# Gated cross-attention: probabilities and attended rows turned by VectorE and a DRAM round trip instead of by TensorE

## The reference

```
memory_proj = memory @ W_mem.T                          # 375 x 512 a batch
attn = softmax(x @ memory_proj.T / sqrt(512))           # 112 x 375
memory_context = attn @ memory_proj                     # 112 x 512
gate = sigmoid(concat(x, memory_context) @ W_gate.T + b_gate)
fused = x + gate * memory_context
out = fused * rsqrt(mean(fused^2) + 1e-6) * norm_w
```

## Time and profile before

| | us |
|---|---|
| median of 3 runs | 296.33 (296.28 to 297.29) |
| span of the profiled execution | 294.5 |
| TensorE busy | 287.4 |
| VectorE busy | 190.2 |
| ScalarE busy | 171.9 |
| GpSimd busy | 161.5 |
| DMA packets, share of 16 engines | 51.1% |

### The profile page before, as it was taken

The page is one execution under the profiler, slowest core; times in us unless marked ns, Lnnn a source line. Parts: engine busy times, 40 slices in busy tenths (PEclk is TensorE's granted clock), DMA queues, the critical chain, the costliest instruction groups (busy, mean ns, idle before and its releaser), DMA issues.

```text
span 294.5 us, 4927 instructions
## 1 busy us (share of the span) xinstructions
PE 287.4 (98%) x1639; PEld 251.4 (85%) x1639; DVE 190.2 (65%) x328; ACT 171.9 (58%) x363; POOL 161.5 (55%) x132
## 2 busy tenths in 40 slices
PE   8999999999999999999999999999999999999991
PEld 4989888888899988888899988888889998888881
DVE  3897556787663267687674247777667335787755
ACT  4886757667447555657636555757735656555442
POOL 0002774859828535858945545685981943555312
PEclk9999999999999999999999999999999999999998
DMA  7997357557452634637472550757654233543101
GB/s 277 421 353 233 116 202 267 177 180 241 137 172 71 250 107 123 236 119 255 160 248 71 175 188 25 266 177 235 208 172 147 102 111 106 179 153 97 38 36 71
DMA packets 15571, 50.83 MB, mean 173 GB/s; under 512 B 1729, under 2 KB 1985, under 8 KB 15297
## 3 DMA queue, kind: packets, MB, share of 16 engines
q1 hardware_dynamic: 15552, 50.60, 51.1%
HBM read 43.25 MB, written 7.34 MB: 172 GB/s over the span
## 4 chain that ended last, share of the span: by engine, by line
PE 98%; issue 0%; DVE 0%; DVEq 0%; POOL 0%; POOLq 0%; ACT 0%
PE gate_ps L283 14%; PE gate_ps L285 14%; PE gate_ps L290 13%; PE ctx_ps L290 5%; PE ctx_ps L283 5%; PE ctx_ps L285 5%; PE q_ps L290 4%; PE q_ps L285 4%; PE q_ps L283 4%; PE am_bank L290 4%; PE am_bank L285 4%; PE am_bank L283 4%; PE score_ps L283 4%; PE score_ps L290 4%; PE score_ps L285 4%; PE pT_ps L335 3%
## 5 line engine op out<-in xcount | busy, mean ns | idle before, releaser
L855 POOL TENSOR_TENSOR memT_lo<-mems_raw,memT_hi 128x752 fp32r<-128x752 f32 x30 | 56.2, 1873 | 75.6 <-ACT memT_hi L513 75.6
L855 POOL TENSOR_TENSOR mem_lo<-mems_raw,mem_hi 128x768 fp32r<-128x768 f32 x30 | 56.2, 1873 | 3.5 <-ACT mem_hi L513 3.5
L638 ACT ACTIVATE am<-am_bank,share 112x256 f32<-112x256 f32 x32 | 15.2, 475 | 44.7 <-PE am_bank L290 44.7
L716 DVE SCALAR_TENSOR_TENSOR work<-work,x_rows 128x512 f32<-128x512 f32 (+1 forms) x29 | 40.6, 1404 | 0.6
L670 DVE TENSOR_TENSOR pT_lo<-pT_ps,pT_hi 128x336 fp32r<-128x336 f32 x32 | 16.2, 508 | 35.8 <-ACT pT_hi L513 35.8
L724 DVE SCALAR_TENSOR_TENSOR work<-work,rstd,norm_w 128x512 f32<-128x512 f32 (+1 forms) x29 | 35.2, 1217 | 1.0 <-POOL rstd L916 1.0
L283 PE MATMUL gate_ps<-wgx_hi,xT_hi 128*128 128x512 f32 x112 | 32.5, 399 | 0.0
L285 PE MATMUL gate_ps<-wgx_lo,xT_hi 128*128 128x512 f32 x112 | 31.7, 391 | 0.0
L290 PE MATMUL gate_ps<-wgx_hi,xT_lo 128*128 128x512 f32 x112 | 31.6, 391 | 0.0
L538 ACT ACTIVATE probs<-score_ps,shift 112x375 f32<-112x375 f32 x32 | 18.4, 574 | 22.4 <-DVE shift L684 22.3
L873 POOL TENSOR_TENSOR guarded<-meansq,eps 128x1 f32<-128x1 f32 x27 | 5.1, 189 | 45.9 <-ACT work L545 45.9
(11 more groups left out here) (123 smaller groups left out, 653.1 us busy)
## 6 DMA issues: line engine op xcount, KB each, us to landing
mems_raw<-in_mems SPq DMA_DIRECT2D x32, 760.0 KB, 4.5
x_rows<-in_x SPq DMA_DIRECT2D x28, 256.0 KB, 4.9
out<-work SPq DMA_DIRECT2D x27, 256.0 KB, 5.0
xT_raw<-in_xT SPq DMA_DIRECT2D x7, 640.0 KB, 5.7
xT_raw<-in_xT SPq DMA_DIRECT2D x3, 512.0 KB, 5.1
work<-in_wgT SPq DMA_DIRECT2D x1, 1024.0 KB, 7.2
x_rows<-in_wgT SPq DMA_DIRECT2D x1, 1024.0 KB, 10.3
xT_raw<-in_xT SPq DMA_DIRECT2D x2, 320.0 KB, 5.0
```

What stands on the lines that cost most here:

```text
L716: dve.scalar_tensor_tensor(out=h[:, t % 2, cols], in0=u[:, cols], scalar=0.5, in1=x_rows[:, t % X_SLOTS, cols], op0=ALU.mult, op1=ALU.add) ...
L855: return pool.tensor_tensor(out, in_, high.bitcast(F32), ALU.subtract)
```

## The change

TensorE's five transposing matmuls a batch, the identity, and their PSUM bank are gone. The turn is made in these steps:

1. ScalarE writes the probabilities to `probs`, now 128 rows with the last 16 zero, in one buffer.
2. VectorE turns each 32 x 32 block in place of the whole matrix (`turn_p`, one instruction over 128 x 384), and lays the blocks out by their new row (`blocks_p`).
3. SyncE writes `blocks_p` to DRAM, waits until it has landed, and reads it back with the blocks placed (`write_p`, `read_p`). A packet of the read is 96 floats, 384 bytes, 512 of them.
4. ScalarE and VectorE take the high and the low part, now from `pT_raw` in SBUF, 128 x 384.

The attended rows go the same way (`turn_am`, `write_am`, `read_am`, 128 x 256; 256-byte packets), their result is 128 columns wide and overlaps the next batch's columns by 16. The order of keys and of memory features inside each chunk of 128 is permuted on the host, so that the block order of the turn fits.

The program is written as steps, all unrolled. Step s has the score of batch s, the x part of the gate two tiles ahead (a third gate bank takes the freed PSUM bank), whole q pieces, gate and context of tile s - 4, and only then `attend` of batch s - 1. The attended rows of batch s - 2 are scaled and turned in step s, and split in step s + 1. The memory comes in two DMAs, keys of either layout apart, each on its own wait. The first four batches and their weight splits are ordered by hand; the zeros for TensorE's first matmuls lie in `blocks_p`; the squares are written over `z`.

The core of the diff, with what is left out marked:

```diff
-        pT_ps = pb("pT_ps", [P, D])
...
-        gate_ps = [pb(f"gate_ps{i}", [P, D]) for i in range(2)]
+        gate_ps = [pb(f"gate_ps{i}", [P, D]) for i in range(3)]
...
-            def load_memory_after(n, slot):
-                sp.wait_ge(memT_lo_ready, n + 1)
-                sp.wait_ge(mem_lo_ready, n + 1)
-                load_memory(n + 2, slot)
+            def load_memT(n):
+                if n >= 2:
+                    sp.wait_ge(memT_lo_ready, n - 1)
+                sp.dma_start(memT_raw[:, n % 2], memT_d[n]).then_inc(memT_loaded[n % 2], 16)
...
+            def write_p(n):
+                sp.wait_ge(blocks_p_ready, n + 1)
+                sp.dma_start(turned_p_d[n % 2], blocks_p[:]).then_inc(p_written, 16)
+            def read_p(n):
+                sp.wait_ge(p_written, 16 * (n + 1))
+                if n >= 1:
+                    sp.wait_ge(pT_lo_ready, n)
+                sp.dma_start(pT_flat, turned_p_d[n % 2].rearrange("(q i) (j n) -> (i j) q n", q=Q, j=Q)).then_inc(p_read, 16)
...
+            for s in range(OPENING, STEPS):
+                if tile_at(s - 2) is not None:
+                    finish(tile_at(s - 2))
+                if s - 2 < BATCHES:
+                    write_am(s - 2)
+                    read_am(s - 2)
+                if s < BATCHES:
+                    write_p(s)
+                if s + 2 < BATCHES:
+                    load_memT(s + 2)
+                if s + 1 < BATCHES:
+                    load_mem(s + 1)
+                if s < BATCHES:
+                    read_p(s)
+                if x_load_at(s) is not None and s != 2:
+                    load_xT(*x_load_at(s))
...
-            def probs_turn(g, b):
-                pe.wait_ge(probs_ready, GROUP * g + b + 1)
-                for c in range(KC):
-                    mm = pe.transpose(probsT[:, c], probs[:, b % 2, c * P:(c + 1) * P], ident[0:ROWS, 0:ROWS])
-                mm.then_inc(pT_done, 1)
...
+            q_piece(0, 1, 1)
+            score(0)
+            wga_chunk(0)
+            wga_chunk(1)
+            score(1)
+            wga_chunk(2)
+            wga_chunk(3)
+            score(2)
+            gate_x(0)
+            attend(0)
+            q_piece(0, 2, 0)
+            score(3)
+            attend(1)
+            q_piece(0, 2, 1)
+            gate_x(1)
+            attend(2)
+
+            for s in range(OPENING, STEPS):
+                t = tile_at(s)
+                if s < BATCHES:
+                    score(s)
+                if t is not None and t + 2 < ALL_TILES:
+                    gate_x(t + 2)
+                if s == BATCHES:
+                    attend(s - 1)
+                for g, unit, half in q_pieces_at(s):
+                    q_piece(g, unit, half)
+                if t is not None:
+                    gate_am(t)
+                    if t < LAST:
+                        context(t)
+                if s < BATCHES:
+                    attend(s - 1)
...
+            for s in range(OPENING, STEPS):
+                t, before = tile_at(s), tile_at(s - 1)
+                if s - 2 < BATCHES:
+                    attended(s - 2)
+                if s - 3 < BATCHES:
+                    amT_high(s - 3)
+                if s + 1 < BATCHES:
+                    split_memT(s + 1)
+                if s < BATCHES:
+                    exponentials(s)
+                if s - 1 < BATCHES:
+                    pT_high(s - 1)
...
+            def turn_p(n):
+                dve.wait_ge(probs_ready, n + 1)
+                if n > 0:
+                    dve.wait_ge(p_written, 16 * n)
+                dve.transpose(turned_p, probs_blocks).then_inc(blocks_p_ready, 1)
...
+                if s - 2 < BATCHES:
+                    turn_am(s - 2)
+                if s - 3 < BATCHES:
+                    amT_low(s - 3)
+                if s < BATCHES:
+                    maximum(s)
+                if before is not None:
+                    fuse(before)
+                if s < BATCHES:
+                    turn_p(s)
+                    shares(s)
+                if s - 1 < BATCHES:
+                    pT_low(s - 1)
+                for g, unit, half in q_pieces_at(s):
+                    q_low(g, unit, half)
+                if t is not None and t < LAST:
+                    add_bias(t)
+                    if before is not None:
+                        norm(before)
+                    gate_context(t)
```

More of the change, by code:

```diff
@@ L38 @@
 TILES = COLS // P
+ALL_TILES = GROUPS * TILES
 DC, EC = D // P, E // P
@@ L50 @@
 X_SLOTS = 4
+Q, R = 4, 32
+TILE_LAG = 4
+STEPS = BATCHES + TILE_LAG - 1
+OPENING = 4
+LAST = ALL_TILES - 1
 def unit_of(batch):
-    end = (batch + 1) * ROWS
+    end = (batch % GROUP + 1) * ROWS
     return next(u for u, (c, n) in enumerate(UNITS) if end <= c + n)
@@ L661, in _ @@
-            group(0, False, first=True)
-            with act.Fori(1, GROUPS - 1) as g:
-                group(g, False)
-            group(GROUPS - 1, True)
+            split_memT(2)
+            split_mem(0)
+            exponentials(1)
+            for i in range(DC):
+                wgx_high(i)
+            exponentials(2)
+            pT_high(0)
+            split_xT(0, 2)
+            split_mem(1)
+            wga_high(0)
+            wga_high(1)
+            attended(0)
+            pT_high(1)
@@ L846, in _ @@
-            group(0, False, first=True)
-            with dve.Fori(1, GROUPS - 1) as g:
-                group(g, False)
-            group(GROUPS - 1, True)
+            wga_low(0)
+            wga_low(1)
+            turn_am(0)
+            pT_low(1)
+            wmT_low(0)
+            wmT_low(1)
+            q_low(0, 2, 0)
+            maximum(3)
+            turn_p(3)
+            shares(3)
+            turn_am(1)
+            pT_low(2)
+            amT_low(0)
+            q_low(0, 2, 1)
+            for s in range(OPENING, STEPS):
+                t, before = tile_at(s), tile_at(s - 1)
+                if s - 2 < BATCHES:
[6 more added lines that the diff above has]
+                    fuse(before)
+                if s < BATCHES:
+                    turn_p(s)
+                    shares(s)
+                if s - 1 < BATCHES:
+                    pT_low(s - 1)
+                for g, unit, half in q_pieces_at(s):
+                    q_low(g, unit, half)
+                if t is not None and t < LAST:
+                    add_bias(t)
+                    if before is not None:
+                        norm(before)
+                    gate_context(t)
+                elif before is not None and t is None:
+                    norm(before)
@@ L903, in _ @@
-            group(0, False, first=True)
-            with pool.Fori(1, GROUPS - 1) as g:
-                group(g, False)
-            group(GROUPS - 1, True)
+            pool.wait_ge(memT_lo_ready, 1)
+            split_memT(1)
+            split_memT(2)
+            split_mem(0)
+            split_mem(1)
+            split_memT(3)
+            split_mem(2)
+            split_memT(4)
+            split_mem(3)
+            for s in range(OPENING, STEPS):
+                before = tile_at(s - 1)
+                if s + 1 < BATCHES:
+                    split_memT(s + 1)
+                if before is not None:
+                    inverse_rms(before)
+                if s < BATCHES:
+                    split_mem(s)
+                if x_unit_at(s) is not None:
+                    split_xT(*x_unit_at(s))
```

732 lines of the change are left out of this document (324 added, 408 removed).

## The result

The changed kernel takes 339.69 us (337.99 to 342.63, 4 runs) against 296.33 (4 runs): ratio 1.1466, 95% interval 1.1409 to 1.1522. The forecast was 293.0 in 286 to 307. It is wrong in sign, and the measured time lies above every rival.

The account below looks back on a forecast made before the run. TensorE was taken as the bound, busy 287.4 of 294.5 us. 294.5 - 15.4 (transposes) + 6 (opening) + 4 (tail) + 2 (in-order waits) = 291.1 us of span, plus 1.8 for the runs' median: 293, range 286 to 307.

Parts of the forecast that it names:

- TensorE's share: TensorE's transposes go: 32 batches x (0.29 + 0.19) us, 15.4 us off the chain; a group of 8 batches takes 65.5 us.
- VectorE: VectorE's load with block transposes and SBUF subtractions: 62.0 us of a 65.5 us group with waits for GpSimd, 52.4 without.
- rival 3: VectorE becomes the bound through dear transposes and waits, 72.6 us a group: 313 us, with half of it 299; chance 0.12.
- DMA work: Work of the DMA engines: 150 us grows to 217 by bytes, or 288 at 51 ns a short packet.
- rival 2: SyncE's chain, waiting for landings before reads, sets the pace: 9.2 us a batch, 317 us, half 303; chance 0.20.
- SyncE's cycle: SyncE's queue per batch, issues and landings: 7.0 us against 8.2, with 3.1 for the attended write and 2.4 for the probabilities'.
- The data's time: Turned data return before TensorE asks; most of both round trips is hidden, about 1 us of slack in a step.
- between the ends: In-order waits in the middle of the run, such as a late landing delaying ScalarE's exponential: 2 us, 0 to 10.
- Opening: Stalls at the start for weight splits, the third unit's low part and the fourth batch's memory: 6 us, 1 to 10.
- Tail: At the end the last attended rows' round trip takes 9.3 us, with 5.6 us of TensorE work to fill it: 4 us, 2 to 7.

Follow-up runs that it names:

- no_trips: Changed kernel without either exchange over DRAM; the readers take the block-turned buffers straight after VectorE's transposes, with more slots; 293.85 us.
- bulk_behind: Changed kernel, SyncE reordered: attended write, x load, store, xT load, attended read, probabilities' write, memory loads, probabilities' read; 315.58 us.
- late_reads: Changed kernel with both reads one step later, ahead of that step's writes, and the attended rows' high and low parts later on ScalarE and VectorE; 313.34 us.
- bulk_behind_xt_last: As bulk_behind, but the xT load stays last in the step, in front of the next attended write; 314.47 us.
- late_reads_bulk_last: As late_reads, with the store and the x load behind both writes on SyncE; 322.70 us.
- no_p_trip: Changed kernel without the probabilities' exchange over DRAM; the attended rows still make theirs; 295.11 us.
- late_am_read: Changed kernel with only the attended read one step later, and the attended rows' high and low parts later on ScalarE and VectorE; 322.58 us.

## Why the prediction was wrong, step by step

- **TensorE's share** (-15.4 us, a group of 65.5): right. no_trips has 65.50 us stretches with TensorE busy for 64.46, and its time, 293.85, is about that forecast for the whole, though without the exchanges.
- **VectorE**: its bound (rival 3) never came. The block transposes took 577 and 434 ns (forecast 560 and 420). The low parts took 703 and 728 ns, not 1.1 us with the wait for GpSimd; in no_trips, closely packed, `amT_lo` took 1114 and 843 ns and `pT_lo` 533 to 631. A group there asked VectorE for 53 to 56 us, between the 52.4 without and the 62.0 with the wait. VectorE's groups by shape, beside the earlier trace rows:

```profile
L754 DVE SCALAR_TENSOR_TENSOR work<-work,rstd,norm_w 128x512 f32<-128x512 f32 x27 | 42.2, 1564 | 2.2 <-POOL rstd L894 1.5
L690 DVE TENSOR_TENSOR amT_lo<-amT_raw,amT_hi 128x256 fp32r<-128x256 f32 x32 | 23.3, 728 | 12.3 <-ACT amT_hi L534 12.3
L690 DVE TENSOR_TENSOR pT_lo<-pT_raw,pT_hi 128x384 fp32r<-128x384 f32 x32 | 22.5, 703 | 24.4 <-ACT pT_hi L534 24.2
L746 DVE SCALAR_TENSOR_TENSOR work<-work,x_rows 128x512 f32<-128x512 f32 x27 | 22.0, 814 | 0.0
L710 DVE STREAM_TRANSPOSE blocks_p<-probs 128x384 f32<-128x384 f32 x32 | 18.5, 577 | 36.4 <-ACT probs L563 32.9 <-DMA turned_p<-blocks_p 3.1
```

- **DMA work** (217 us, 288 at the upper bound): 68.7% of 337.3 = 232 us, so the exchanges added 82 us where 67 were forecast. Packets of 256 and 384 bytes took 18 and 22 ns on the median, those of 1024 bytes 46 (by the packet records); rival 2's reason, 51 ns each, was wrong. The Trainium skill, "DMA: Bandwidth & Descriptors", section "Specifications", asks for 512 bytes at least for full rate, with a read-modify-write below. The trace agrees in part: by these times a byte in a packet of 256 costs 1.6 times one in a packet of 1024, and no run here shows whether a read-modify-write is the reason.
- **SyncE's cycle** (7.0 us against 8.2): this step failed. The probabilities' write was priced right (2.3 us against 2.4, of which 1.0 is waited for), the attended write was put at 3.1 and landed in 4.7 on the median and over 8 behind an xT load. Its sum had the 512 KB directly ahead and not the 760 KB of memory, 192 KB of short packets and up to 640 KB of xT, part of which was still in the 16 engines; without the memory it did land in 3.0. Between the 4th and the 32nd score SyncE waits for landings for 149.9 us, 5.4 a batch, of which 4.6 are the attended write's; the issues of a batch, 0.32 to 0.67 us apiece, 7 or 8 of them, add 3.4, and its other waits 14.0 us in all, 0.5 a batch: 9.3 of the 9.60 us. With its issue the attended write takes 5.0 us of the cycle on the mean, 1.9 more than the 3.1, out of 2.6 by which the cycle was too short.
- **The data's time** ("most of both round trips is hidden by the longer lag"): failed too, for ScalarE. It was judged by when TensorE asks, and ScalarE asks far earlier, with the exponential of the next batch behind it in order. The loop, as the step shown above has it, is: attended write lands late, memory load and probabilities' write go out late, ScalarE waits for either read or for the memory, exponential, transpose, write. VectorE is in it too: its low part of the attended rows, 1.77 us at 166.89, stands ahead of the maximum. The 2 us "between the ends" (0 to 10) were 37.7.
- **Opening** (6 us, 1 to 10): 5.61 us for `wgx_lo` (2.4 in no_trips) and 2.08 for `memT_lo`, 7.7, inside the range; the 4th score comes 3.8 us later than in no_trips. **Tail** (4, 2 to 7): stalls of 0.88 and 1.75 us for the last two tiles, and one of 2.73 before the last attention, which the sum didn't have; 5.4 together, 4.2 more than no_trips behind the 32nd score. The size was right, the place in part.
- **The clock**: not priced at all. TensorE is busy for 290.9 us against 275.0 in no_trips with the same 1479 matmuls, mean granted clock 0.955 and 0.992. So of the 45.7 us, 16 are longer busy time of the same matmuls, as at 163.92 with the clock at its lower level, and 30 are idle time. Here the waiting cost half as much again.
- **Rival 2** named the place and the sign; at 9.2 us a batch its cycle was near the measured 9.60, but by luck: it came from 51 ns a packet, and its time, 317, is 23 us short. Its chance of 0.20 was too low: the sum left 1.2 us of slack in 8.2 and I gave its terms, all from landings in a busy queue, no margin.

Shown: that the exchanges are the cost and together far more than apart; that 24 to 26 of the 46 us go by order alone, with every byte the same, either with the attended write ahead of the bulk (bulk_behind) or with the reads a step later (late_reads). Argued only: that the last 20 us are in-order waits for transfers in shared DMA engines. Every order tried moved them, and none gave the memory a third slot, which would loosen ScalarE's wait for `memT_raw`; so the cause of this rest stays open. No version with both exchanges beats the kernel before; the best is late_reads at 1.0583, with bulk_behind_xt_last at 1.0592 level with it. By no_trips, an exchange that cost nothing would bring 0.9% in all.

## What to carry to other kernels

Before a write and its read back are put in a queue that issues everything, add up all bytes that the shared DMA engines may still hold when the write is issued, not only those of the neighbouring rows, and price the wait at its worst step. Don't wait for a landing with nothing to issue meanwhile: here it was as good to put the write ahead of the bulk (315.6 and 314.5 us) as to read a step later (313.3). Judge "in time" by the first in-order engine that asks, and by what stands behind it there, not by the engine that is the bound.

## What the runs showed of the hardware that I had not expected

- The same 128 KB write landed in 2.2 to 2.4 us on the median in late_reads_bulk_last, no_p_trip and late_am_read and in 4.7 us in the changed kernel. Other queues did not cure it: with ScalarE issuing the bulk it took 5.3 us; with GpSimd issuing the write 2.8, but its read then 3.5.
- An issue of a write took SyncE 0.32 to 0.35 us after a wait (turned_p at 54.06, turned_am at 57.14) and 0.43 to 0.51 us close behind another issue (168.43, 164.80).
- The same subtraction of 256 elements a lane took 404 ns on the median in late_reads and 1.77 us in the changed kernel at 166.89, where GpSimd's 3.40 us subtraction from 164.99 was under way. `fuse` went from 1476 to 814 ns on the mean with the same operands; that the phases of the two engines moved is the likely reason and not shown.
